# Cross-attention stage: keys of four sequences in one product, values as fp32r products, queries in halves, a new order on all engines, and a new order at the last two items

## The reference, cut to what matters

```python
# cross-attention, 8 heads of 64
xn = layernorm(x)
q, k, v = xn @ Wq, context @ Wk, context @ Wv
x = x + softmax(q k^T / 8) v @ Wo + bo
# then, on layernorm(x), two layers of local attention and a gated feed-forward part
qkv = shift_token(x) @ wqkv
x = x + local_attention(rotary(l2norm(q)), rotary(l2norm(k)), v) @ wo
h = layernorm(shift_token(x)) * lg + lb
a, g = split(h @ w1 + b1)
x = x + (a * gelu(g)) @ w2 + b2
```

## Time and profile before

| | |
|---|---|
| median of 3 runs | 1491.39 us (1489.23 to 1492.93) |
| the profiled execution's own time | 1492.72 us |
| its span in the profile | 1490.9 us |
| mean granted TensorE clock | 0.993 of full speed |
| busy: PE / DVE / ACT / POOL | 1438.4 / 1102.3 / 937.8 / 760.3 us |
| X phase | from 0 to about 300 us |
| L phase | from about 300 us to the end |

### The profile page before, as it was taken

The page is one execution under the profiler, slowest core; times in us unless marked ns, Lnnn a source line. Parts: engine busy times, 40 slices in busy tenths (PEclk is TensorE's granted clock), DMA queues, the critical chain, the costliest instruction groups (busy, mean ns, idle before and its releaser), DMA issues.

```text
span 1490.9 us, 33891 instructions
## 1 busy us (share of the span) xinstructions
PE 1438.4 (96%) x11913; PEld 1276.8 (86%) x11913; DVE 1102.3 (74%) x3053; ACT 937.8 (63%) x2672; POOL 760.3 (51%) x577
## 2 busy tenths in 40 slices
PE   7999999998999999999999999899999999999986
PEld 6788888877889888888888888788888888888876
DVE  3766666456888787788877877887788888887864
ACT  2766666535666666666666667666666666666661
POOL 1121112044666566666665665765566655666632
PEclk9999999999999999999999999999999999999998
DMA  6211111200010100000000021011111111111000
GB/s 195 99 53 61 45 52 52 86 30 19 29 35 28 29 28 28 27 27 27 27 27 28 28 70 38 23 36 39 41 46 36 34 34 34 34 41 34 29 29 30
DMA packets 50821, 62.90 MB, mean 42 GB/s; under 512 B 8514, under 2 KB 32424, under 8 KB 50728
## 3 DMA queue, kind: packets, MB, share of 16 engines
q1 hardware_dynamic: 50728, 61.68, 13.0%
HBM read 37.86 MB, written 16.78 MB: 37 GB/s over the span
## 4 chain that ended last, share of the span: by engine, by line
PE 73%; DVE 12%; ACT 4%; issue 4%; POOL 2%; DMA 2%; SPq 2%; DVEq 0%; POOLq 0%; ACTq 0%
PE pb L520 33%; PE pb L820 6%; PE pb L806 6%; PE pb L782 5%; PE pb L751 5%; PE pb L766 5%; PE pb L844 4%; PE pb L586 2%; DVE p_t L1390 2%; PE pb L574 2%; PE pb L624 2%; PE pb L628 2%; DMA x<-x 1%; DVE p_t L1404 1%; DVE r_sin L1377 1%
## 5 line engine op out<-in xcount | busy, mean ns | idle before, releaser
L1579 POOL TENSOR_TENSOR n_inv<-n_cl,half_neg 128x16 f32<-128x16 f32 x64 | 210.9, 3295 | 177.7 <-DVE n_cl L1362 174.2
L1083 ACT ACTIVATE p_t<-p_t,s_nm 128x128 f32<-128x128 f32 (+1 forms) x512 | 227.0, 448 | 26.6 <-DVE s_nm L1390 25.1
L520 PE MATMUL pb<-h_hi,w_hi 128*128 128x256 f32 x704 | 208.3, 296 | 2.8 <-DVE h_lo L1353 2.4
L520 PE MATMUL pb<-h_hi,w_lo 128*128 128x256 f32 x704 | 199.3, 283 | 0.0
L520 PE MATMUL pb<-h_lo,w_hi 128*128 128x256 f32 x704 | 199.3, 283 | 0.0
L1584 POOL TENSOR_TENSOR r_cos<-r_cos,r_sin 128x1024 f32<-128x1024 f32 x64 | 154.4, 2413 | 58.1 <-DVE r_sin L1377 58.1
L1074 ACT ACTIVATE pt_t<-pb 128x512 f32<-128x512 f32 x192 | 114.4, 597 | 101.3 <-PE pb L766 100.4
L1390 DVE CUSTOM_DVE_ANT_0 p_t<-pb,mask_t 128x128 f32<-128x128 f32 (+1 forms) x512 | 152.0, 353 | 26.1 <-PE pb L751 25.6
L1610 POOL TENSOR_TENSOR hg_lo<-hg,hg_hi 128x256 fp32r<-128x256 f32 x192 | 141.6, 758 | 54.4 <-DVE hg_hi L1421 54.4
L1041 ACT ACTIVATE qk_sq<-pb 128x512 f32<-128x512 f32 x128 | 72.3, 591 | 152.9 <-PE pb L520 152.9
L520 PE MATMUL pb<-wqkv_hi,xt_hi 128*128 128x512 f32 x384 | 164.2, 428 | 3.4 <-DVE r_sin L1377 3.1
(11 more groups left out here) (136 smaller groups left out, 4042.0 us busy)
## 6 DMA issues: line engine op xcount, KB each, us to landing
y_state<-x SPq DMA_DIRECT2D x32, 256.0 KB, 2.1
x_cur<-y_state SPq DMA_DIRECT2D x32, 256.0 KB, 2.6
x_res<-y_state SPq DMA_DIRECT2D x32, 256.0 KB, 2.7
x_in<-x SPq DMA_DIRECT2D x16, 256.0 KB, 2.8
x_state<-x SPq DMA_DIRECT2D x16, 256.0 KB, 2.0
x_orig<-x_state SPq DMA_DIRECT2D x16, 256.0 KB, 2.9
out<-x SPq DMA_DIRECT2D x16, 256.0 KB, 2.2
x<-x SPq DMA_DIRECT2D x32, 112.0 KB, 2.3
```

The source lines that it names most:

```text
L520: mm = pe.matmul(dst, s, m, start=(n == 0 and k == 0), stop=(n == len(pairs) - 1 and k == 2))
L1083: e = nc.scalar.activation(pu, pu, ACT.Exp, bias=s_nm[:, j, k:k + 1], scale=-1.0, accum_out=s_sum[:, j, k:k + 1])
L1579: nc.gpsimd.tensor_tensor(n_inv[:, t], n_cl[:, t], half_neg[:], ALU.pow).then_inc(pool_inv, 1)
```

## The change

**Keys and values.** The context comes already transposed from the host, channels on partitions and all sequences side by side; channels 128 to 191 stand twice, in partitions 0 to 63 and 64 to 127 of the second chunk, and so do the rows of the key and value weights. ACT rounds a group of four sequences (308 columns) at once, DVE makes the rests; in the second chunk's upper half the rounded rows are replaced by their rests. So hi and lo of the last 64 channels share one full-height matmul, and a product takes 5 fp32r matmuls instead of 6. The keys are made one chunk of 128 for four sequences at a time, one chunk per iteration for the next group, the values once per sequence:

```diff
-                for c in range(IC):
-                    for k in range(2):
-                        mm = pe.matmul(pb[:, 6, c * P:c * P + CTX], xk_w[:, k, c * P:c * P + P], c_t[:, k, :],
-                                       start=(k == 0), stop=(k == 1))
...
+            def x_keys(group, c, b):
+                pe.wait_ge(c_rest, group + 1)
+                u, cols = group % 2, slice(c * P, c * P + P)
+                over_context(pb[:, b, 0:GCTX], [(xk_hi[:, 0, cols], c_hi[:, u, 0]), (xk_hi[:, 0, cols], c_lo[:, u]),
+                                                (xk_lo[:, 0, cols], c_hi[:, u, 0]), (xk_hi[:, 1, cols], c_hi[:, u, 1]),
+                                                (xk_lo[:, 1, cols], c_hi[:, u, 1])]).then_inc(x_pk, 1)
...
+            def x_values_of(a):
+                if a == 0:
+                    pe.wait_ge(w_lo, WEIGHT["xv"])
+                u, cols = a // GROUP % 2, slice(a % GROUP * CTX, (a % GROUP + 1) * CTX)
+                over_context(pb[0:CTX, 7, :], [(c_hi[:, u, 0, cols], xv_hi[:, 0]), (c_hi[:, u, 0, cols], xv_lo[:, 0]),
+                                               (c_lo[:, u, cols], xv_hi[:, 0]), (c_hi[:, u, 1, cols], xv_hi[:, 1]),
+                                               (c_hi[:, u, 1, cols], xv_lo[:, 1])]).then_inc(x_pv, 1)
```

```diff
+                if g == 0:
+                    idle_products(8, 7)
+                    x_turn(0)
+                    idle_products(13, 7)
                     pe.wait_ge(w_lo, WEIGHT["xq"])
+                    x_queries(0, 0)
+                    x_queries(0, 1)
+                    pe.wait_ge(w_lo, WEIGHT["xk"])
+                    for c in range(IC):
+                        x_keys(0, c, FIRST_KEYS[c])
+                    x_values_of(0)
+                    x_turn(1)
+                    return
                 if b is not None:
                     x_scores(b, was, 0)
+                if a is not None:
+                    x_queries(a, 0)
...
                 if d is not None:
                     x_out(a, d)
-                if a is not None:
-                    x_queries(a)
-                if isinstance(g, int) and g < 2:
-                    idle_products(50 if g == 0 else 30, 7)
+                if g == 1:
+                    idle_products(12, 7)
                 if b is not None:
                     x_scores(b, was, 1)
                     x_probs(b, 0)
+                if a is not None:
+                    x_values_of(a)
+                    x_queries(a, 1)
...
                     x_probs(b, 1)
...
+                if next_keys(a):
+                    x_keys(*next_keys(a), 6)
...
                     x_probs(b, 2)
...
                     x_probs(b, 3)
+                if a is not None and a < SEQS - 1:
+                    x_turn(a + 1)
...
                     for t in range(NT):
                         x_values(b, was, t)
```

```diff
+                if a is not None and a < SEQS - 1:
+                    deviation(x_mv[:, 0, :, 1], x_ve[:, 0], x_rs[:, 0], a + 1, x_bmv, a + 2, x_eps, x_rst)
...
+                if d is not None and d < SEQS - 2:
+                    pool.wait_ge(x_res1, d + 1)
+                    x_bias_rows(d + 2, par)
                 if d is not None:
...
+                    deviation(x_mv[:, 1, :, 1], x_ve[:, 1], x_rs[:, 1], d, y_bmv, d + 1, y_eps, y_rst)
```

**Between the phases.** `xt_hi` and `xt_lo` now share memory with the context tiles, so their zero column is written at the end of the X phase, in POOL's stream behind the last deviation of y, and PE waits for it:

```diff
             def between(g):
                 if g == 0:
-                    pe.wait_ge(w_lo, WEIGHT["w10"])
+                    pe.wait_ge(w_lo, WEIGHT["w10c"])
+                    pe.wait_ge(zero_made, 1)
...
+            pool.wait_ge(x_pv, SEQS)
+            nc.gpsimd.memset(xt_hi[:, T:T + 1].bitcast(F32), 0.0)
+            nc.gpsimd.memset(xt_lo[:, T:T + 1].bitcast(F32), 0.0)
             nc.gpsimd.memset(x1[:, 0, 1], 0.0)
             nc.gpsimd.memset(hg_hi[:, FC - 1].bitcast(F32), 1.0).then_inc(zero_made, 1)
```

**Layer 1's third iteration.** POOL makes two of the three rests of w1 ahead of the deviation, the third right behind it:

```diff
+                if isinstance(g, int) and g == SEQS + 2:
+                    next_w1(0)
+                    next_w1(1)
+                if c is not None and not last_norm:
                     deviation(l_mv[:, :, 1], l_ve[:], l_rs[:], c, dve_bmv, at(c, 1, 1), pool_eps, pool_rst)
+                if isinstance(g, int) and g == SEQS + 2:
+                    next_w1(2)
                 if a is not None:
                     add_parts(a, 0)
-                    if isinstance(g, int) and g == SEQS + 2:
-                        for k in range(3):
-                            next_w1(k)
```

**The last items.** In iteration 32 PE does both halves of item 31's output product before all six hidden chunks of item 30; DVE and POOL do item 31's statistics and normalisation among item 30's gates. In iteration 33 PE turns item 31, feeds item 30's chunks and makes item 31's hidden chunks in the order 0, 1, 5, 2, 3, 4; the chunk that goes through the small DMAs is the third:

```diff
+        LAST_CHUNKS = [0, 1, FC - 1] + list(range(2, FC - 1))
...
+                if last_norm:
+                    turn_h(b, c)
+                    for m in range(FC - 1):
+                        feed(c, d, m)
+                    hidden(a, b, c, 0)
+                    hidden(a, b, c, 1)
+                    feed(c, d, FC - 1)
+                    for m in gate_chunks(c)[2:]:
+                        hidden(a, b, c, m)
+                    return
...
+                if last_attention:
+                    for m in range(FC):
+                        hidden(a, b, c, m)
```

More of the change, by code:

```diff
@@ L233, in build @@
         zero_made = sem("zero_made")
-        x_load, c_load = [sem(f"x_load{u}") for u in range(2)], [sem(f"c_load{u}") for u in range(2)]
+        norm_made = sem("norm_made")
+        x_load, c_load = [sem(f"x_load{u}") for u in range(2)], sem("c_load")
         x_bst, x_bmv = sem("x_bst"), sem("x_bmv")
@@ L278, in one, with x_iterations, next_keys @@
             return t[bass.ds(n, 1)].rearrange("o p t d -> p (o t) d")
-        def x_iterations(eng, run):
-            for g in range(3):
+        def x_iterations(run):
+            for g in range(SEQS + 2):
                 run(g)
-            with eng.Fori(1, SEQS // 2 - 1) as i:
-                for u in range(2):
-                    run((i, u + 1))
-            for g in range(SEQS - 1, SEQS + 2):
-                run(g)
+        def next_keys(a):
+            return ((a - 1) // GROUP + 1, (a - 1) % GROUP) if a is not None and 1 <= a <= SEQS - GROUP else None
         def x_roles(g):
@@ L322, in has_next, with is_last, gate_chunks, place @@
             return a is not None and not (isinstance(a, int) and a == ITEMS - 1)
+        LAST_CHUNKS = [0, 1, FC - 1] + list(range(2, FC - 1))
+        def is_last(n):
+            return isinstance(n, int) and n == ITEMS - 1
+        def gate_chunks(n):
+            return LAST_CHUNKS if is_last(n) else list(range(FC))
+        def place(n, m):
+            return gate_chunks(n).index(m)
+        def gates_of(n, m, share):
+            order = gate_chunks(n)
+            return max([k + 1 for k in range(place(n, m)) if share[order[k]] == share[m]], default=0)
         QKV_PLACE = {(0, 1): 1, (0, 0): 2, (0, 2): 3, (1, 0): 4, (1, 1): 5, (1, 2): 6}
         W1_BANK = [4, 0, 1, 2, 4, 0]
+        GL_PLACE = [m % 3 for m in range(FC)]
         S_BANK = [3, 4, 3, 4, 3, 4]
@@ L443, in _ @@
-            for g in range(SEQS - 3, SEQS + 2):
-                run_x(g)
+            x_iterations(run_x)
             second, third = slice(TAIL, 2 * TAIL), slice(2 * TAIL + 1, 3 * TAIL + 1)
@@ L894, in run_l @@
                     turn_p(a, b, d, 3)
-                if c is not None:
+                if c is not None and not last_attention:
                     hidden(a, b, c, 0)
@@ L1112, in run_l @@
                 a, b, c, d, par = l_roles(g)
+                last_attention = isinstance(g, int) and g == ITEMS
                 if a is not None:
@@ L1142, in run_l @@
                     copy_v(a, 1, par)
+                if last_attention:
+                    probs_copy(b, 5)
+                    out_hi(b)
+                if isinstance(g, int) and g == ITEMS + 1:
+                    for m in gate_chunks(c):
+                        gelu(c, m, layer)
+                    return
                 if c is not None:
@@ L1145, in run_l @@
                     next_weights(g, 0)
-                if b is not None:
+                if b is not None and not last_attention:
                     probs_copy(b, 5)
@@ new lines, in x_residual, with y_stats @@
+            def x_residual(d, par):
+                dve.wait_ge(x_wo, at(d, 1, 1))
+                dve.wait_ge(x_bias, at(d, 1, 1))
+                if later(d):
+                    dve.wait_ge(x1_store, at(plus(d, -1), 16, 16))
+                nc.vector.tensor_tensor(x1_x.rearrange("p t d -> p (t d)"), pb[:, 1],
+                                        x_b[:, par].rearrange("p t d -> p (t d)"), ALU.add).then_inc(x_res1, 1)
+            def y_stats(d):
+                dve.wait_ge(x_res1, at(d, 1, 1))
+                for t in range(NT):
+                    e = nc.vector.bn_stats(x_st[:, 1, t], x1_x[:, t])
+                e.then_inc(y_bst, 1)
@@ L1410, in gate @@
                 rows = P if m < FC - 1 else TAIL
-                dve.wait_ge(act_gelu, at(c, FC, m + 1))
-                if m == 0 and later(c):
+                dve.wait_ge(act_gelu, at(c, FC, place(c, m) + 1))
+                if place(c, m) == 0 and later(c):
```

(3 more changed lines are left out.)

539 lines of the change are left out of this document (310 added, 229 removed).

## The result

The changed kernel takes **1456.3 us** (median of 5 runs, 1456.18 to 1459.72) beside 1490.16 us for the kernel before on the same chip: ratio 0.978, interval 0.976 to 0.979. The forecast was 1451 us, with 1437 to 1466 as its range: the direction and the order of the terms by size were right, and the gain came out 5 us smaller than forecast. The profiled execution took 1456.24 us, with a span of 1454.1 against 1490.9.

A forecast was written before the change was run, and what follows sets the result against it. PE's instructions were taken to bound the X phase and most of the L phase, loads the start. Terms -16.7 - 13.5 + 4.5 - 5.8 - 9 = -40.5 us gave 1451 us, range 1437 to 1466.

The forecast's parts named there:

- forecast case: Whole kernel: all the forecast's terms together give 1451 us; chance 0.78.
- moved collision: X iterations: POOL's bias rows now slow DVE's normalisation of x, adding 0.7 us to the pace (bounds 0 and 0.95).
- Pace of the X iterations: X iterations 2 to 15: PE needs 14.2 us each instead of 16.41; with the collision the pace is 14.9.
- the chains of ACT and DVE: Rival, X phase: these chains set the pace at 15.7 us or more, total 1466 us; chance 0.10.
- fp32r runs at the full rate: Contrary rival, key and value products: they run at the old 0.43 us pitch, total 1460 us; chance 0.04.
- the clock stays at 1.00: Contrary rival, X iterations: waits make PE's clock fall in every one, total 1508 us; chance 0.03.
- Layer weights and context groups: X iterations: weight pieces expose 0.4 us in nine iterations, 3.6 us; tables and two context groups add about 0.9.
- The start: Before X iteration 2: no wait for constants, so it starts at 36.6 instead of 50.1 us, -13.5 (bounds -10, -17).
- the lower clock: Start, iteration 1: PE runs slower after waiting some 6 us, adding 1.3 us.
- Between the phases: X to L phase: PE waits for the zero column, then a slow first projection; +4.5 us (bounds +3.2, +5.5).
- Layer 1's third iteration: L phase: two of POOL's three w1 rests move off DVE's normalisation of h; -5.8 us (bounds -3, -7).
- The last items: Kernel's end: hidden chunks go behind the output product and the last chunk skips the DMAs; -9 us (bounds -6, -11).

The follow-up runs named there:

- run 1: Changed kernel with POOL's bias rows given a third buffer and run first in the iteration, not beside x's normalisation; ratio 0.974 to the kernel before.
- run 2: Changed kernel with DVE's rests of layer weights moved ahead of the rest of the turned x; ratio 0.9735 to the kernel before.
- Run 3: Changed kernel with context group 1 rounded and its rests taken in the middle of iteration 1, not at iteration 0's end; ratio 0.979 to the kernel before.
- run 4: Changed kernel with context group 1 handled mid-iteration 1 and x of sequence 2 loaded ahead of the first layer weights; ratio 0.9747 to the kernel before.
- run 9: Changed kernel with keys and values as two plain float32 products each instead of five fp32r, their rests left out; ratio 0.979 to the kernel before.

## Why the prediction was right, and where its sizes were off

The forecast case came: X phase bound at 14.9 by the moved collision, a new wait between the phases, gains in the start, in layer 1 and at the end. Two of its terms were mis-sized, the layer weights and the start; the others held or were off by some 2 us at most. Step by step:

- **Pace of the X iterations.** PE's instructions 14.2, measured 14.13 (run 1); with the collision 14.9, measured 14.84. Right, and the collision's share (0.7 us) too. The rivals on this step fall: the chains of ACT and DVE allow 14.13, fp32r runs at the full rate, the clock stays at 1.00 in iterations 2 to 15.
- **Layer weights and context groups.** This is one of the two terms that failed. I took 0.4 us for each of nine pieces and 0.9 for tables and groups, 4.5 in all; it was 10.1 (there are eight pieces, at 0.88 on average, groups 2.0, tables 1.0), less 1.2 for iteration 15, which has no next x. I had laid out only the wait before the output product (0.44, as in the row above). The same 1.22 us also stand ahead of maxima 0, and so of the exponentials; DVE waits for these itself, and its residual and maxima 2 come 0.85 us later (rows of iterations 8 and 10). A delay at the head of DVE's queue was priced for one of those that wait for it. That DVE's place costs the whole is shown by run 2; the path is read from the rows.
- **The start.** -10.6 against -13.5. The first maxima came when I said, 24.55, and for the reason that I gave. What failed is behind it, in two places. I listed the context's load as the only late one, and left out x of sequence 2, which SP issues behind the first layer weights and for which DVE's statistics wait 1.61 us, until 28.23. And I priced the lower clock at 1.3 us; from 29.48 on it cost 2.5 (10.06 us instead of 7.54). Run 3, taken alone, could be read as if the context's load did no harm; run 4 shows what the two loads give together, clock included, and leaves open what x alone would give. Scores 0 came 1.2 us late, of which PE's wait of 0.75 for x normalised beside two bias rows (2.67 instead of 0.73 us) is the larger part; the first maxima came on time all the same. No run takes the gain of 10.6 us itself apart into the order of the loads, the prologue and the rest.
- **Between the phases.** +4.5, measured +3.1 in the changed kernel's profile, +4.4 to +4.7 in seven others and +5.6 in run 9. Right, the slow projection included.
- **Layer 1's third iteration.** -5.8, measured -6.2. Right.
- **The last items.** -9, measured -6.9. The residual of item 31 gained 4.9 instead of 5.8, as PE waits 2.34 and 1.42 us there for probabilities and the attention output's rests. Then the turn of item 31 to the end of its hidden products took 13.5 us instead of 11.7: of these 1.8 us, 1.25 are the last chunk of item 30's second product, which now stands among them on PE (0.4), and a wait of 0.85 for a gate, both left out.
- **Luck.** The -3.1 us of scatter in the L phase weren't forecast, and the full clock between the phases in this one profile is worth another 1.3 to 1.6. Without both, the span would have fallen by about 32 us instead of the forecast 40.5, so the number came out closer than the steps. The range of the forecast also stops at 1466, although its bounds add up to 1469.

## What to carry to other kernels

A delay put at the head of an engine's queue must be priced for everyone who waits for that queue in the next stage, not for the first one found; an idle gap of the same engine (here 2.35 us ahead of the turned x) costs nothing instead. Where the pace is the larger of two limits, a cheaper instruction on the engine that isn't the limit shows little (0.17 of 0.88 us), so first find what makes the engine wait, then make its work cheaper. And behind a late load look for the next late one before counting on the gain, and look at the granted clock of the stretch behind it, which was worth about as much here (2.1 of 5.0 us).

## What the runs showed of the hardware

- The clock behind the same wait of 3.58 us isn't the same in every execution: over the 10 us from the first projection on it was granted at 0.78 to 0.91 in eight profiles and at 1.00 in one, and 1.3 to 1.6 us hang on it (2.5 in run 9).
- A normalisation on VectorE of 0.73 us took 1.70 beside one bias row of 1.33 us on GpSimd and 2.67 beside two of 2.58 together; a subtraction of 1.22 took 2.30 beside one of 1.52. VectorE lost about 0.7 of GpSimd's time each time. GpSimd's bias row took 1.33 us there and 1.27 with no VectorE instruction beside it (in the kernel before). What it cost depended on the place: the normalisation's 0.97 us cost 0.7 of pace, more than the wait that PE showed (0.48 to 0.58), and the subtraction's 1.08, in DVE's gap, nothing that shows.
